# GpSimd folds per-position factors into weights: twenty one-input instructions a group in place of eight two-input ones

## What is computed

```python
concat = jnp.concatenate((x, lu, ru, ld, rd), axis=1)      # the image and four shifted copies: 10 channels
normed = (concat - mean) * jax.lax.rsqrt(var + EPS)        # mean and variance per image
normed = normed * gamma[None] + beta[None]                 # a factor and an offset per channel and pixel
y = conv_general_dilated(normed, W, window_strides=(8, 8)) # 8x8 patches: 169 tokens of 128 numbers an image
h = y + b
h = h + attention_over_256_neurons(layernorm(h))           # distances, softmax over inverse distances, values
```

## Time and profile before

| | us |
|---|---|
| three runs, median (lowest to highest) | 3399.97 (3396.25 to 3401.76) |
| the profiled execution, its own time | 3385.79 |
| its span, first to last instruction | 3383.9 |
| mean granted TensorE clock in it | 0.769 |

### The profile page before, as it was taken

How to read it: one execution, slowest core, us unless ns; L and a number is a source line. 1 busy time by engine, 2 the same in 40 slices (tenths; PEclk the granted TensorE clock), 3 DMA queues, 4 the chain that set the end, 5 groups by cost and what they waited for, 6 DMA issues and landing times. The chain is left out here.

```text
span 3383.9 us, 63281 instructions
## 1 busy us (share of the span) xinstructions
PE 2483.1 (73%) x14081; PEld 1880.2 (56%) x14082; DVE 2187.2 (65%) x7770; ACT 1658.6 (49%) x4362; POOL 2434.6 (72%) x2518
## 2 busy tenths in 40 slices
PE   5999995788777757666766377787787787777773
PEld 4877774454444434333433166676676676666663
DVE  5999997688876767767765444444444444577775
ACT  5988886556554545545543033333333333333332
POOL 4777772077777777777777777777777777777776
PEclk8999998567665676766665579878878878777886
DMA  8877872133333333333333154444444444699996
GB/s 304 285 262 264 268 266 102 35 98 105 104 104 95 101 96 96 100 96 99 98 97 96 63 135 128 128 126 114 112 113 112 111 112 113 212 303 302 303 303 214
DMA packets 401951, 522.41 MB, mean 154 GB/s; under 512 B 65661, under 2 KB 329555, under 8 KB 390579
## 3 DMA queue, kind: packets, MB, share of 16 engines
q1 hardware_dynamic: 318610, 373.60, 37.2%
q0 software_dynamic: 83232, 147.75, 12.9%
HBM read 257.02 MB, written 264.08 MB: 154 GB/s over the span
## 5 line engine op out<-in xcount | busy, mean ns | idle before, releaser
L1109 POOL DMA_INDIRECT ytk<-yo,idxy x1080 | 1055.8, 978 | 329.4 <-issue 324.2
L1100 POOL DMA_INDIRECT xed<-xr,idxs x1014 | 998.3, 985 | 392.0 <-issue 308.1
L1520 ACT ACTIVATE yo<-wide,gi 128x128 f32<-128x128 f32 x1080 | 307.8, 368 | 865.1 <-DMA ytk<-yo,idxy 836.5
L1372 PE MATMUL wide<-wdt,hT 64*128 x2160 | 376.0, 324 | 184.1 <-DVE hT L1877 181.1
L1868 DVE SCALAR_TENSOR_TENSOR ae<-the,bank 128x256 f32<-128x256 f32 x270 | 113.5, 420 | 604.1 <-ACT the L1511 590.9
L1354 PE MATMUL bank<-wgu,xeT 128*128 x2160 | 370.1, 325 | 140.8 <-ACT xeT L1505 138.1
L1372 PEld LDWEIGHTS wide<-wdt,hT 64*128 64x128 f32 x2160 | 316.9, 222 | 235.2 <-issue 232.1
L1354 PEld LDWEIGHTS bank<-wgu,xeT 128*128 128x128 f32 x2160 | 330.8, 234 | 182.2 <-issue 181.6
L594 POOL TENSOR_TENSOR weff<-w,gam 128x384 f32<-128x384 f32 x338 | 268.8, 830 | 10.1 <-DMA tokb<-in_tokb 8.7
L1282 PE MATMUL wide<-xn,e 128*128 128x128 f32 (+3 forms) x1024 | 274.2, 391 | 1.6 <-ACT e L1442 1.6
L1290 PE MATMUL wide<-ident,xr 128*128 128x128 f32 x169 | 44.6, 414 | 250.4 <-DVE xr L1613 250.4
(11 more groups left out here) (334 smaller groups left out, 5060.1 us busy)
## 6 DMA issues: line engine op xcount, KB each, us to landing
xin<-xed SPq DMA_DIRECT2D x1080, 74.0 KB
ytk<-zeros SPq DMA_DIRECT2D x42, 1536.0 KB, 9.6
yg<-ytk SPq DMA_DIRECT2D x42, 1536.0 KB, 7.9
xs<-in_xcol SPq DMA_DIRECT2D x42, 1280.0 KB, 6.7
ytk<-yo,idxy POOLq DMA_INDIRECT x1080
xed<-xr,idxs POOLq DMA_INDIRECT x1014
H<-in_ximg SPq DMA_DIRECT2D x4, 2704.0 KB, 22.1
h1d<-H SPq DMA_DIRECT2D x42, 256.0 KB, 9.5
```

Source lines behind the costliest of these rows:

```text
L1100: p.indirect_dma_start(xed[:, :], bass.IndirectOffsetOnAxis(ap=idxs[:, slot, j, k:k + 1], axis=0), xr[:, slot, j, :], None).then_inc(scat[ ...
L1109: p.indirect_dma_start(ytk[:, :], bass.IndirectOffsetOnAxis(ap=idxy[:, slot, j:j + 1], axis=0), yo[:, slot % ES, j, :], None)\
L1372: last = pe.matmul(eO[slot % 2][:, j * D:(j + 1) * D], hT[:, slot % 2, j, :], wdt[:, bass.ds(e, 1), :].rearrange("p o f -> p (o f)"), star ...
L1520: last = a.activation(yo[:, slot % ES, j, :], eO[slot % 2][:, j * D:(j + 1) * D], ACT.Copy, scale=gi[:, slot, j, 0:1])
```

## The change

The four positions' factors are first copied by one GpSimd `tensor_copy` (128 x 20) to a new small buffer `gams`, whose address does not depend on the loop's counter. Then one `tensor_scalar` for each position and context (128 x 128) multiplies the weights by a factor that is read as one number per partition. Between the copy and the products stands a wait for the copy's own semaphore. The other engines' code is not touched.

```diff
+        gams = sb("gams", [128, 2, TG, NCTX])
...
+        gams_ready = sem("gams_ready")
...
                     nj = tiles_of(g)
+                    p.tensor_copy(gams[:, slot, 0:nj, :], gam[:, bass.ds(TG * g, nj), :]).then_inc(gams_ready, 1)
                     after(p, conv_done, g - 1)
+                    p.wait_ge(gams_ready, g + 1)
+                    p.nop(nofuse=True)
                     for j in range(nj):
-                        for k0, k1 in ((0, 3), (3, NCTX)):
-                            ins = p.tensor_tensor(
-                                weff[:, slot, j, k0:k1, :], w5[:, k0:k1, :],
-                                gam[:, bass.ds(TG * g + j, 1), k0:k1].rearrange("p o c -> p (o c)").unsqueeze(2)
-                                .to_broadcast([128, k1 - k0, 128]), ALU.mult)
+                        for k in range(NCTX):
+                            ins = p.tensor_scalar(weff[:, slot, j, k, :], w5[:, k, :], gams[:, slot, j, k:k + 1], None, ALU.mult)
                     ins.then_inc(weff_ready, 1)
```

## The result

The changed kernel takes 3570.08 us (median of 5 runs, 3557.87 to 3575.74) against 3399.48 for the kernel before in the same comparison: a ratio of **1.0497, 95% interval 1.0481 to 1.0513**, 170 us slower. The profiled execution took 3557.87 us, its span is 3556.0 against 3383.9, 172.1 longer. So the time went the way of rival B, and further than its upper end.

The account below looks back on a forecast made before the run. DVE's instruction list was taken as the bound, with `fold` staying in POOL's room. DVE's gain of -13.5 and the beginning's +1.0 made -12.5, rounded to -12 us: 3388 us from a median of 3399.97, range 3368 to 3450.

Parts of the forecast that it names:

- rival B: POOL becomes the bound, `scale` comes late and DVE waits at L814: +36 us at 0.45 spacing, +132 at 0.57; chance 0.26.
- The bound and the room: In the steady first stage DVE's instruction list is the bound; POOL idles 3.1 us a group, giving `fold` 9.56 us.
- the limit of 0.405 us spacing: Start-to-start spacing of the twenty products at which `fold` has used up its room: (9.56 - 1.46)/20.
- one hold-up of POOL by DVE: In `fold`, 1.0 us a group lost to one L814, within 6.0 + 0.46 + 1.0 = 7.5 us.
- the first of the parts: The products in `fold`: eight instructions go, twenty `tensor_scalar` come, spaced 0.30 us, 6.0 us in all.
- The small extra read: Reading one factor per partition in each `tensor_scalar`: 0.09 us at most, about half of it taken.
- The upper bound: Spacing of a `tensor_scalar` at most 0.57 us, from a two-input 128 x 256 with twice the elements.
- The sum of 0.43 us: Spacing by the skill's rules: 1.8 cycles an element, the read command and a start of about 0.15; rival B by about +20 us.
- The gain on DVE: DVE's losses to `fold` fall from 0.83 to 0.45 us a group, over the stage 31 to 17.5: gain 13.5 us.
- each meeting costs half of one POOL instruction: A DVE instruction meeting `fold` waits 0.15 us on average, half of 0.30; L814, L797 and L800 all meet it.
- The beginning: fold(1), ahead of the second convolution, takes 6.46 us instead of 5.44: +1.0 us once, +6.4 at 0.57 spacing.

Follow-up runs that it names:

- twenty products: Against the kernel before: the copy and its wait, then twenty two-input products of 128x128 in place of eight larger ones; ratio 1.0003, no difference.
- half width: Against the changed kernel: the twenty tensor_scalar on 64 of the 128 outputs each, half of the products left out; 4560.03 us, 53 over the kernel before.
- wide: Against the changed kernel: one tensor_scalar of 128x640 for each position, four contexts' factors left out; 3367.43 us, 22 under the kernel before.
- half kernel: Against the changed kernel: tensor_scalar for two of a group's four positions only, the others left out; 3358.27 us, 31 under the kernel before.

## Why the prediction was wrong, point by point

- **The bound and the room were right.** DVE set the pace, POOL had 3.1 us of room a group, but the limit of 0.405 us spacing was a little high: at 0.36 (twenty products) the period was 11.89 us, but at 0.414 (half width) already 12.86. The forecast counted one hold-up of POOL by DVE where a longer `fold` meets two. With both the limit is (11.86 - 2.3 - 0.37 - 1.7)/20 = 0.375 us.
- **The step that failed is the first of the parts: "I take ... 0.30 us, near the lower end because the affine select is the nearest in shape and kind".** Measured: 0.58. The rows at 0.24 to 0.26 us were a copy with conversion and a select, and their price was taken over to an operation that costs more for each element: 2.6 ns against the 0.8 of a copy and the 1.64 of a two-input product of `fold`. The small extra read, on which that part spent its care, was right (0.08).
- **The upper bound was no bound.** It assumed that a one-input instruction can't cost more than a two-input one of twice the elements. It costs slightly more (0.58 against 0.57).
- **Rival B's mechanism was the one that came**, with `scale` late and DVE waiting before L814. Its price at 0.57, +132 us, is 38 short of 170. With the limit at 0.375 and the spacing at 0.58 the same sum is 20 x 0.205 x 40 = 164 us, against the 159.7 measured from the first `scale` to the last; the start costs 12.9 more.
- Of the Trainium skill's two rules one held. The read command of about 102 cycles (GPSIMD Engine Reference, Performance pitfalls for Q7 kernels), an estimated 0.085 us, agrees with the 0.08 measured here. The 1.8 cycles an element as the best of a plain loop (the same page, Elementwise — side-by-side cycle accounting) would be an estimated 1.5 ns; the `tensor_scalar` takes 2.6 and the copy about 0.8, so it is neither's price. The sum of 0.43 us fell on the right side of the limit with an element price that was too low.
- **The gain on DVE was real and was paid for elsewhere.** It was forecast at 0.34 us a group; in the changed kernel DVE's two-input instructions lose nothing, worth 0.80 us a group as the wide and the half kernel show. That it is nothing is owed to where they arrive. The gain went under in 4.1 us of longer period. The rule that each meeting costs half of one POOL instruction was wrong too: a `tensor_scalar` of 0.58 us keeps DVE out for 0.22 us at most, whereas a product of 0.36 us keeps it out for 0.25, and DVE sometimes waited for several.
- The beginning was put at +1.0 us, or +6.4 at the upper bound; it is 12.9. The second convolution starts 6.7 us later (61.92 in place of 55.24), as the upper bound had it. The forecast left out that fold(2) and fold(3) also stand ahead of the first `scale`, which now follows them without the 6.1 us of waiting that it had before.

## What to carry to other kernels

A new kind of instruction has to be priced per element and per instruction of its own kind; neither the number of inputs nor a relative with a similar name bounds it, and an upper bound taken from another operation is a guess. Before taking work off an engine that waits, write down its room a group and the unit price at which the room is gone; here one undisturbed fold of 20 instructions would have decided it. Where a second engine is slowed by whatever it happens to meet, look at where inside that instruction it arrives, and change only the piece that it meets: one of the eight products replaced by two `tensor_scalar`, with the copy, gave 27 us, all eight replaced cost 170.

## What was not expected of the hardware

- GpSimd, f32, start to start, for n elements a partition: copy 0.13 + 0.00083 n us, two-input product (second input broadcast) 0.155 + 0.00164 n, `tensor_scalar` with a factor per partition 0.25 + 0.0026 n. One input was dearer than two.
- A GpSimd `tensor_scalar` keeps out a VectorE instruction with two SBUF inputs for its first part only: 0.22 us of 0.58 at 128 elements (0.14 with a constant), 0.64 of 1.86 at 640, the last from one meeting. A copy or a two-input product does so for all but its last 0.1 us. In the other direction a large instruction of VectorE holds up the next instruction of GpSimd, by 0.85 us in the changed kernel, but not a `tensor_scalar` that is past its first part. The Trainium skill (SBUF — State Buffer, Who interferes with whom) has the first of the two block the other for a whole instruction. Copies and products come near that, and the runs with `tensor_scalar` contradict it. That the first part is the reading of the input, and the rest computing, would fit the copy's 0.83 ns an element (0.64 - 0.22 = 0.42 us for 512 elements more) against 2.6 in all, and is only argued.
- VectorE isn't always let in at the next boundary between GpSimd's instructions: one L810 of 28 waited 1.74 us with products of 0.36 us, twelve 0.7.
